# Work of the second spline phase begun in the causal phase, three-instruction Newton steps, and products that nobody reads moved between the picks

## The reference, cut to what matters

```python
x = x + 0.5 * L0_ffn(layernorm(x))      # 8 experts, each token goes to one
x = x + L0_attn(layernorm(x))           # 16 heads, relative positions, own layernorm
x = x + 0.5 * L0_ffn(layernorm(x))
x = x + 0.5 * L1_ffn(layernorm(x))      # the first spline phase
x = x + L1_attn(layernorm(x))           # the causal phase
x = x + 0.5 * L1_ffn(layernorm(x))      # the second spline phase
return x
```

## Time and profile before

| | |
|---|---|
| median of 3 runs | 770.83 us (769.11 to 771.67) |
| the profiled execution | 764.29 us, span 762.6 us |
| TensorE products | 588.3 us, 77% of the span |
| VectorE | 530.6 us, 70% |
| ScalarE | 440.1 us, 58% |
| GpSimd | 210.1 us, 28% |
| TensorE's granted clock, mean | 0.887 of full speed |

### The profile page before, as it was taken

The page is one execution under the profiler, slowest core; times in us unless marked ns, Lnnn a source line. Parts: engine busy times, 40 slices in busy tenths (PEclk is TensorE's granted clock), DMA queues, the critical chain, the costliest instruction groups (busy, mean ns, idle before and its releaser), DMA issues. The chain is left out here.

```text
span 762.6 us, 16796 instructions
## 1 busy us (share of the span) xinstructions
PE 588.3 (77%) x5268; PEld 411.2 (54%) x5268; DVE 530.6 (70%) x1872; ACT 440.1 (58%) x952; POOL 210.1 (28%) x264
## 2 busy tenths in 40 slices
PE   4369947738999999999999998353994881787880
PEld 3258933225566666667676666242984451365560
DVE  7513245826778787999999995872225899866897
ACT  3225524327788888888888885651551543464522
POOL 1714415101930680096040000043442200312100
PEclk9999977878999999999999999655998785999875
DMA  9958826899999999999974421724553000000001
GB/s 249 259 165 288 272 80 188 257 311 322 290 347 333 239 302 384 238 216 308 337 172 133 113 65 64 197 82 143 180 173 94 0 1 0 0 1 1 0 1 55
DMA packets 130450, 130.80 MB, mean 172 GB/s; under 512 B 27148, under 2 KB 106876, under 8 KB 129468
## 3 DMA queue, kind: packets, MB, share of 16 engines
q1 hardware_dynamic: 121628, 101.88, 48.7%
q0 software_dynamic: 4032, 25.73, 9.1%
q10 hardware_dynamic: 4704, 2.11, 1.1%
HBM read 73.43 MB, written 52.92 MB: 166 GB/s over the span
## 5 line engine op out<-in xcount | busy, mean ns | idle before, releaser
L1528 DVE CUSTOM_DVE_ANT_0 l0am_prob<-l0am_ps_s,l0am_bias 128x512 f32<-128x512 f32 x256 | 161.6, 688 | 48.2 <-PE l0am_ps_s L1605 36.4
L1448 ACT ACTIVATE l0am_prob<-l0am_prob,l0am_neg_top 128x512 f32<-128x512 f32 x256 | 172.2, 729 | 12.6 <-DVE l0am_neg_top L1528 12.6
L1617 PE MATMUL l0am_ps_t<-c_ident,l0am_prob 128*128 128x128 f32 x1024 | 137.8, 278 | 0.0
L1617 PEld LDWEIGHTS l0am_ps_t<-c_ident,l0am_prob 128*128 128x128 f32 x1024 | 113.4, 142 | 16.7 <-issue 15.8
L613 ACT ACTIVATE l0f_h<-l0f_psU,l0f_experts 128x128 f32<-128x128 f32 x184 | 52.7, 369 | 80.2 <-PE l0f_psU L908 80.2
L1442 ACT COPY l0am_probT<-l0am_ps_t 128x512 f32<-128x512 f32 x128 | 69.1, 591 | 44.2 <-PE l0am_ps_t L1617 44.2
L1605 PE MATMUL l0am_ps_s<-l0am_ks,l0am_qs 32*128 32x512 f32 x512 | 73.9, 647 | 15.3 <-DVE l0am_neg_top L1528 13.1
L1515 DVE COPY l0am_probT<-l0am_ps_t 128x512 f32<-128x512 f32 x128 | 82.1, 683 | 2.2 <-PE l0am_ps_t L1617 2.1
L786 DVE COPY l0f_xsT<-l0f_psT 128x128 f32<-128x128 f32 x46 | 13.4, 292 | 86.6 <-PE l0f_psT L898 86.6
L1630 PE MATMUL l0am_ps_c<-l0am_probT,l0am_v 128*9 128x128 f32 x2048 | 67.9, 273 | 0.9 <-issue 0.9
L524 POOL DMA_INDIRECT token_results<-l0f_ys,l0f_token_i x46 | 44.4, 965 | 77.1 <-DVE l0f_ys L796 76.5
(11 more groups left out here) (317 smaller groups left out, 980.3 us busy)
## 6 DMA issues: line engine op xcount, KB each, us to landing
l0am_bias<-near_terms SPq DMA_DIRECT2D x128, 192.0 KB, 5.5
near_terms<-l0am_near POOLq DMA_DIRECT2D x6, 3072.0 KB, 13.2
l0f_mine<-l0f_experts SPq DMA_DIRECT2D x46, 256.0 KB, 2.8
near_terms<-l0am_near SPq DMA_DIRECT2D x2, 3072.0 KB, 11.2
l0am_rows_k<-position_k SPq DMA_DIRECT2D x12, 448.0 KB, 8.8
position_q<-l0am_rows SPq DMA_DIRECT2D x20, 224.0 KB, 5.3
position_k<-l0am_rows SPq DMA_DIRECT2D x20, 224.0 KB, 5.2
l0f_experts<-in_L_ffn_w SPq DMA_DIRECT2D x2, 2048.0 KB, 8.8
```

What stands on the lines that cost most here:

```text
L1448: nc.scalar.activation(prob[:, k, :], prob[:, k, :], ACT.Exp, bias=neg_top[:, k:k + 1], scale=-1.0)\
L1528: dve.tensor_tensor_reduce(out=prob[:, k, :], in0=ps_s[:, j, :], in1=bias[:, j, at:at + S], scale=-1.0, scalar=HUGE, op0=ALU.add, op1=ALU.min,
L1617: last = pe.transpose(ps_t[:, u % 2, i, :], prob[:, u % SLOTS_, i * P:(i + 1) * P], ident[:, :])
```

## The change

Three things are changed.

First, the opening of a spline phase (statistics, first estimate, Newton step, first normalised tiles) becomes a class, `SplineOpening`, with semaphores and tables of its own. The first spline phase uses it inside the phase. For the second one it is made ahead of the causal phase, and the causal phase issues a part of it: VectorE takes the statistics of batch 0 in the loop's second turn and of batch 1 in its third, between `bias_values(b + 1)` and `weigh(b + 1, 0)`. In the last turn VectorE does the Newton step of half 0 and normalises tiles 4 to 7 ahead of `add_y(3)`, and ScalarE, at the end of its list, makes the first estimate and normalises tiles 0 to 3. In the second spline phase only the statistics of batches 2 and 3 and what belongs to half 1 are left, and TensorE's three opening products (`keep_busy`) are left out. In the first spline phase tiles 0 to 3 are now normalised by ScalarE too.

Second, a Newton step takes three instructions in place of four, in every phase: with r the estimate, (var + eps) r, then that times -0.5 r, then (that + 1.5) r.

Third, in both spline phases `keep_busy` ahead of `compress` asks for 2 products in place of 4, and a new `keep_busy` of 2 stands between `pick_parameters(1)` and `turn_hots(2)`.

```diff
-                    done(dve.tensor_tensor(newton[:, 2, tiles], newton[:, 1, tiles], newton[:, 1, tiles], ALU.mult))
-                    done(dve.scalar_tensor_tensor(newton[:, 3, tiles], mv[:, tiles, 1], 1e-5, newton[:, 2, tiles], ALU.add, ALU.mult))
-                    done(dve.tensor_scalar(newton[:, 4, tiles], newton[:, 3, tiles], -0.5, 1.5, ALU.mult, ALU.add))
-                    done(dve.tensor_tensor(newton[:, 5, tiles], newton[:, 1, tiles], newton[:, 4, tiles], ALU.mult))
+                    done(dve.scalar_tensor_tensor(newton[:, 2, tiles], mv[:, tiles, 1], 1e-5, newton[:, 1, tiles], ALU.add, ALU.mult))
+                    done(dve.scalar_tensor_tensor(newton[:, 3, tiles], newton[:, 2, tiles], -0.5, newton[:, 1, tiles], ALU.mult, ALU.mult))
+                    done(dve.scalar_tensor_tensor(newton[:, 5, tiles], newton[:, 3, tiles], 1.5, newton[:, 1, tiles], ALU.add, ALU.mult))
```

The same stands at five more places (L1488, L1752, L2061, L2391 and the class below). The class and its use:

```diff
+class SplineOpening:
+    HALF = TILES // 2
...
+    def statistics(self, dve, g):
+        tiles = range(4 * g, 4 * g + 4)
+        for t in tiles:
+            last = dve.bn_stats(self.stats[:, t, :], self.x[:, t, :])
+        self.done(last)
+        for t in tiles:
+            last = dve.bn_aggr(self.mv[:, t, :], self.stats[:, t, :])
+        last.then_inc(self.var_ready, 1)
+
+    def deviate(self, act, h):
+        ts, newton = self.half_of(h), self.newton
+        act.wait_ge(self.var_ready, 2 * h + 2)
...
+    def refine(self, dve, h):
...
+        dve.wait_ge(self.std_ready, h + 1)
...
+        dve.scalar_tensor_tensor(newton[:, 6, ts], mv[:, ts, 0], -1.0, newton[:, 5, ts], ALU.mult, ALU.mult).then_inc(self.mean_ready, 1)
+
+    def normalise_by_vector(self, dve):
+        for t in range(4, self.HALF):
+            dve.tensor_scalar(self.xn[:, t, :], self.x[:, t, :], self.mv[:, t, 0:1], self.newton[:, 5, t:t + 1],
+                              ALU.subtract, ALU.mult).then_inc(self.xn_by_dve, 1)
+
+    def normalise_by_scalar(self, act, h):
+        act.wait_ge(self.mean_ready, h + 1)
+        for t in (range(4), range(self.HALF, TILES))[h]:
+            self.nc.scalar.activation(self.xn[:, t, :], self.x[:, t, :], ACT.Identity, bias=self.newton[:, 6, t:t + 1],
+                                      scale=self.newton[:, 5, t:t + 1]).then_inc(self.xn_by_act, 1)
...
@@ spline_phase, GpSimd: the last of four adds of beta @@
-                        pool.wait_ge(mean_ready, 1)
+                        pool.wait_ge(opening.mean_ready, 2)
@@ spline_phase, ScalarE @@
                 nc.scalar.preload_act_table_set("natural_log_exp_and_others")
-                deviate(0, (var_ready, 2), log_ready, std_ready, newton, mv)
+                if not opened:
+                    opening.deviate(act, 0)
+                    opening.normalise_by_scalar(act, 0)
                 copy_xnT(0)
                 copy_xnT(1)
-                deviate(1, (var_ready, 4), log_ready, std_ready, newton, mv)
+                opening.deviate(act, 1)
                 decay_clusters(0)
                 decay_clusters(1)
...
+                opening.normalise_by_scalar(act, 1)
@@ spline_phase, VectorE @@
-                for g in range(3):
-                    statistics(range(4 * g, 4 * g + 4), x, stats, mv).then_inc(var_ready, 1)
...
+                opening.start_vector(dve)
+                if not opened:
+                    for g in range(3):
+                        opening.statistics(dve, g)
+                    opening.refine(dve, 0)
+                    opening.normalise_by_vector(dve)
+                else:
+                    opening.statistics(dve, 2)
+                opening.statistics(dve, 3)
+                opening.refine(dve, 1)
@@ spline_phase, TensorE @@
-                keep_busy(pe, banks[:, 6, :], c["ident"], x, 3)
+                if not opened:
+                    keep_busy(pe, banks[:, 6, :], c["ident"], x, 3)
...
                 pe.wait_ge(picks_ready, 1)
-                keep_busy(pe, banks[:, 6, :], c["ident"], x, 4)
+                keep_busy(pe, banks[:, 6, :], c["ident"], x, 2)
                 compress()
                 pe.wait_ge(picks_ready, 2)
                 keep_busy(pe, banks[:, 6, :], c["ident"], x, 4)
...
                 pick_parameters(1)
+                keep_busy(pe, banks[:, 6, :], c["ident"], x, 2)
                 turn_hots(2)
@@ causal_phase, VectorE, in the loop over b @@
                     weigh(b, 3)
                     if b + 1 < B:
                         bias_values(b + 1)
+                        if b:
+                            opening.statistics(dve, b - 1)
                         weigh(b + 1, 0)
+                    else:
+                        opening.refine(dve, 0)
+                        opening.normalise_by_vector(dve)
                     add_y(b)
```

More of the change, by code:

```diff
@@ L1901, in spline_phase @@
+def spline_phase(nc, name, x, consts, lw, opening, opened, out=None):
     c = consts
@@ L2259, in _, with causal_phase @@
                 pick_parameters(3)
-        clear_semaphores(nc, own_sems)
-def causal_phase(nc, name, x, consts, lw):
+        clear_semaphores(nc, own_sems + opening.own_sems)
+def causal_phase(nc, name, x, consts, lw, opening):
     c = consts
@@ L2553, in network @@
             ffn_phase(nc, ctx, "l0f1", x, None, c, weights("L0_ffn_"), (sorted_tokens, token_results), None, layer1, closing)
-        spline_phase(nc, "l1f0", x, c, layer1)
-        causal_phase(nc, "l1a", x, c, layer1)
-        spline_phase(nc, "l1f1", x, c, layer1, out)
+        with ExitStack() as spline_ctx:
+            first = SplineOpening(nc, spline_ctx, "l1f0", x, c)
+            spline_phase(nc, "l1f0", x, c, layer1, first, False)
+        second = SplineOpening(nc, ctx, "l1f1", x, c)
+        causal_phase(nc, "l1a", x, c, layer1, second)
+        spline_phase(nc, "l1f1", x, c, layer1, second, True, out)
 def kernel(**inputs):
```

84 lines of the change are left out of this document (49 added, 35 removed).

## The result

| | before | after |
|---|---|---|
| median, both on one chip | 769.97 us (768.59 to 772.65, 6 runs) | 761.43 us (759.08 to 763.34, 6 runs) |
| ratio | | 0.9901, 95% interval 0.9875 to 0.9926 |
| the profiled execution | 764.29 us, span 762.6 | 760.95 us, span 759.0 |

The kernel is 7.6 us faster by the ratio (5.7 to 9.6), where 9.3 was forecast. The two profiled executions are only 3.6 us of span apart, where the medians are 8.5 apart, so the first question is which stages differ. These are the busy times by stage of the changed kernel (span, busy us and instructions of the engines, granted TensorE clock, DMA share, GB/s), cut at the first instruction of each phase: expert 1, attention, expert 2, first spline, causal, second spline, and at the end the stretch of the second picks.

The account below looks back on a forecast made before the run. VectorE was taken to bound the spline phases, with no single engine bounding the whole. Opening 4.4, Newton steps 4.1 and products 0.8 gave 9.3 us off 770.83, so 761.5 us, range 759.2 to 767.2.

Parts of the forecast that it names:

- Newton steps hidden: Rival: 2.5 us of Newton gain sinks in expert and attention waits; with late half 1 scores, 765.1 us; chance 0.28.
- The profiled execution: Whole kernel: the profiled run falls from 764.29 to 755.0 us, the median staying 6.5 above it.
- The opening: Second spline phase: `plus` 4.85 us earlier, causal phase ending 0.45 later; net gain 4.4 us, between 3.8 and 6.0.
- The late scores of half 1: Second spline phase, second `plus`: at the lower clock these scores could cost 1.1 us; counted as nothing, 1.1 in the range.
- Newton steps: All phases: one instruction less per step, 0.19 to 0.20 us each where on the path; gain 4.1 us, 1.2 to 4.8.
- Tiles 0 to 3 of the first spline phase: Moved to ScalarE: first copy 0.2 to 0.5 us later, VectorE's statistics earlier; counted zero, minus 0.4 to plus 0.5.
- Products: Second spline phase: new unread products keep the clock up, so second picks end before `magnitude(1)` needs them; gain 0.8 us.
- fewer products ahead of `compress` let the clock fall: Lower bound of the products term: the next eight products last up to 7.5 us and hold `turn_hots(0)`; loss of 1.4.
- ScalarE late after the load: Rival, second spline opening: the first copy comes 1.24 us later because of the table load; 762.7 us, chance 0.05.
- A spline phase at the lower clock throughout: Rival: less filling before `compress` slows one spline phase's picks; nine us lost there, 771.3 us, no difference; chance 0.07.
- Both spline phases so: Rival: lower clock throughout both spline phases; 18 us lost, 8.5 gained, about 780 us; chance 0.03.
- It does nothing: Rival: the block's end moves out by as much as the opening moves in; rows leave 1 us for that, not 5.

Follow-up runs that it names:

- newton_early: The kernel before with three-instruction Newton steps in the two expert phases, the attention and its closing alone; 766.63 us, ratio 0.9975.
- opening_only: The kernel before with the moved opening alone, four-instruction Newton steps and unread products as before; 764.86 us, ratio 0.9951.
- vector_first: The changed kernel with VectorE again normalising tiles 0 to 3 of the first spline phase; 762.91 us in one execution.
- kernels with held products: Two unread products added at the end of TensorE's causal list, to the changed kernel (761.15 us, one more at the second spline opening) and in the combined kernel (763.70 us).
- changed_again: The changed kernel unaltered, measured again against the kernel before; 767.14 us, ratio 0.9932.
- together_unheld: The combined kernel without the two unread products at the end of the causal phase, on another chip; 765.07 us, ratio 0.9941 against the kernel before.
- newton_only: The kernel before with three-instruction Newton steps in every phase and nothing else; 764.14 us, ratio 0.9929.
- combined kernel: Changed kernel with four products before `compress`, unread products ending the causal phase, no load in the opened phase, tiles 0 to 3 by VectorE; 763.70 us, ratio 0.9878.
- products_only: The kernel before with the two edits of the unread products alone; 768.06 us, ratio 1.0008.

## Why the prediction was right, point by point

**The whole.** 761.5 forecast, 761.43 measured; gain 9.3 against 7.6 by the ratio, and 5.2 when the changed kernel was measured again (0.9932). So the time was met partly by luck: one kernel's ratio moved by 0.3% between two measurements. The first interval (5.7 to 9.6 us) holds the 9.3; the second (3.1 to 7.5) leaves it out and holds the 5.7 of the rival *Newton steps hidden*. Luck too is that 761.43 meets 761.5 so closely: the forecast was counted from 770.83, and in this comparison the kernel before took 769.97. The sign and the largest term are certain, the second digit of the gain is not.

**The profiled execution** was to become 755.0, because nothing in the change touches what puts the median 6.5 above it. It took 760.95, 0.5 below its median. The 6.5 belonged to the one execution that happened to be profiled and not to the kernel: expert 1 lasted 106.52 there, the shortest of all fourteen.

**The last three phases together** were to lose 6.8 us (0.8 in the first spline phase, 6.05 in the second, less 0.05 that the causal one was to grow). They last 169.76 and 168.82 in two profiles with the old instructions in them (before, newton_early) and 164.39 and 164.57 in the two of the changed kernel: 4.2 to 5.4 less. The 2.5 of the expert and attention phases rest on newton_early alone, 1.9 with an interval that takes in zero.

**The opening, 4.4 forecast.** This was right in its steps. `plus` 4.88 earlier (4.85 forecast), both batches of statistics under ScalarE's softplus (VectorE idle 1.18 behind each), `add_y(3)` at 703.52, 0.35 behind TensorE's last sum, and the next block 0.47 later behind that sum (0.45). That leaves 4.4. The distance from that sum to the next block is 1.38 to 1.43 in the four kernels without the moved opening and 1.84 to 1.85 in the seven with it, short steps and nothing held, so this price does not hang on one execution.

What the forecast took as a choice between two ends changes from one execution to the next. Of the eight profiles with this opening and no held clock, three had the scores of half 0 at the lower level and `plus` at 5.97 or 5.98 (changed, opening_only, vector_first), and five had them at the full one and `plus` at 4.28 to 4.30. So the reason given for the lower clock, TensorE's longer stand without a product, does not settle it: all eight had that stand. Both kernels with held products had the full clock, which with five of eight without them proves little. The full level gave 1.7 us at `plus`, but not all of it stayed: in changed_again the next `plus` came 1.23 us earlier (11.03 against 12.26). And at the full clock not only the scores set `plus`: VectorE's second Newton step, which the forecast had done at 3.9, took 0.66 for its first instruction and began its last at 4.20, and `plus` followed without a pause.

**The late scores of half 1**, which had no term and 1.1 in the range, exist: 1.03 us in together_unheld, 0.61 in the first spline phase of changed_again. The waits stand behind scores of 3.69 and 3.57 us, at the lower clock. None of the four kernels without the moved opening shows one, so whether the change makes them likelier stays open.

**Newton steps, 4.1 forecast.** By time, newton_only gives 5.4 (3.5 to 7.4), and the profiles bear out only a part. Over 11 profiles with three instructions and 3 with four, expert 2 lasted 120.91 against 122.35 on average, 1.4 less, which is the forecast; but single executions spread from 119.08 to 123.31, so this is weak. Firmer is that the phase's first scatter begins 29.7 behind its start on average (28.8 to 30.2) in place of 30.7 (30.6 to 30.9): about 1.0 of the 1.4 is there at that point. Attention: 358.92 against 359.31, 0.4 less in a spread of 4. Expert 1, 0.7 forecast, is not there: 110.12 against 108.46. The trace shows why the step cannot pay there. VectorE's index `pos_i` is ready 0.66 earlier; timeline of before, then of after:

```profile
29.88 0.17 DVE L690 CAST l0f_pos_i<-l0f_pos 128x4 int32<-128x4 f32 x1
```

```profile
29.22 0.17 DVE L689 CAST l0f_pos_i<-l0f_pos 128x4 int32<-128x4 f32 x1
```

But GpSimd issues sixteen scatters 1.26 us apart, and its last began at 36.99 before and at 37.11 after: its queue, and not VectorE's list, sets when the scatters end, and the first results behind them leave at 53.35 before and 53.41 after. In the first spline phase the steps give what was forecast, 0.8: newton_only 53.59 against 54.48 and 54.41. Of the causal phase's 0.4 little is seen: its first turned tiles come 0.2 earlier (3.58 against 3.77 behind the phase's start), but TensorE's last sum ends only 0.06 earlier in the changed kernel (54.11 against 54.17), and the clock's moment moves it by more than that.

**Tiles 0 to 3 of the first spline phase**, "I count zero, minus 0.4 to plus 0.5". This step was mis-sized. ScalarE's 1.66 against VectorE's 1.12 made the first copy late, `plus` came at 9.46 with shorter steps just as it did without them (9.46 before, 9.07 in newton_only), and it then took 0.70 in place of 0.20. Against the combined kernel, whose scores of half 1 were at the full clock as well, `magnitude(0)` came 0.61 later (32.82 against 32.21 behind the phase's start). A second part was not in the forecast: at the step into the causal phase VectorE is idle 1.08 us in place of 0.70. In all, 54.45 against 53.46: 1.0 us lost, and the 0.8 of the steps with it. The 1.08 stands in all six kernels that have both the short steps and ScalarE's tiles, and 0.70 or 0.71 in the other eight. Its cause is open; it appears only with both edits together, and no computing engine ends that block later than VectorE.

**Products, 0.8 forecast.** The mechanism was right, the size was that of one execution. Without the new products `magnitude(1)` waited in two of five kernels (0.78, 0.95); with them in none of nine. With two asked for ahead of `compress`, `magnitude(0)` waited in three of seven (0.41, 0.66, 0.68); with four in none of seven. On average 0.35 gained and 0.25 lost, too little for products_only's interval to tell. The bound "fewer products ahead of `compress` let the clock fall" has these waits for it, at 0.4 to 0.7 rather than 1.4; three of seven against none of seven is a sign and no proof.

**The rivals.** *Newton steps hidden* (765.1) is true for expert 1 and, by another way, for the first spline phase; the late scores that it was joined with stayed out of the second spline phase in both profiles of the changed kernel. With changed_again's 5.2 us it came nearer to the second measurement than the forecast did. *ScalarE late after the load* is out: the copy follows the load by 0.01 us, and without the load it comes at 0.70, when TensorE has turned the tiles. The drain that the Trainium skill, "ScalarE: Activation LUTs", section "What ACT_TABLE_LOAD costs", adds does not appear; but the page gives it for a switch to a different set, and this load named a set already in use. A true switch is in the earlier trace rows, where the next activation follows the load by 0.02, without the drain. *A spline phase at the lower clock throughout* did not occur: in none of the fourteen profiles did both magnitudes of a phase wait. *Both spline phases so* is out by the same rows. *It does nothing* is out by the 5.7 us of the second phase and by both intervals of the changed kernel.

**What stays open.** The combined kernel was 3.4 us below the changed one, while the three last phases of their profiles differ by only 0.8 (163.80 against 164.57). No edit touches the expert and attention phases, and in this pair of profiles they were 5.5 us longer in the combined kernel (595.88 against 590.41), so the rest of the 3.4 is not found in any trace. 0.9878 is the best ratio measured, but 1 us is all that the traces explain, and the kernel without the held products, at 0.9941, does not confirm more.

## What to carry to other kernels

Work that opens a block can be done at the end of the block before, on engines that wait there; read its price as the delay of the engine that ends last, and its worth from the first instruction that the bound engine waits for. A term read from a wait of one execution is worth that wait times how often it occurs: profile the unaltered kernel more than once before an idle time is priced. When an edit takes tiles from the bound engine to another, follow the first consumer of these tiles: it, and not the busy time, sets the gain.

## What the runs showed of the hardware

The same sixteen products took 3.69 us at a granted clock of 0.50 in one execution of a program and 2.00 at 1.00 in another of the same program, after the same instructions: the granted clock's moment is not fixed by the instructions before.

A `scalar_tensor_tensor` over 128x8 that began in the midst of GpSimd's 1.26 us add of 128x512 took 0.61 to 0.67 in place of 0.17 (nine profiles), and a 128x64 `tensor_scalar` 0.53 to 1.15 in place of 0.20; each ended 0.02 to 0.06 us behind the add. Not every instruction is slowed: the four 128x128 `bn_stats` at the head of the block took 0.87 in the changed kernel beside the same adds.

The second spline phase's block opens 0.65 to 0.77 us behind the end of its last engine (VectorE before, ScalarE after, TensorE with held products), so unread products there cost what they outlast the others by, 0.6 here. Other blocks of this program open 0.67 to 1.05 behind. A table load of a set already in use still takes 1.28 us.
